# A graph layer kernel on one core: the first tiles reordered, four weight sums moved, two turned tiles moved to SyncE, and two small regroupings

## The chip, the cores and the metric

The kernel runs on one core of a Trainium2 chip. The metric is the device time of one execution in microseconds (us), measured on the slowest core, here the only one. Lower is better.

## What is computed

The layer takes x (1250 nodes of 1024 numbers) and a list of 20,000 edges. Cut to what matters here:

```python
xn = layernorm(x)
h   = relu(xn @ W_self0 + mean_of_neighbours(xn) @ W_neigh0 + b0)
gnn = h @ W_self1 + mean_of_neighbours(h) @ W_neigh1 + b1
q, k, v = relu(xn @ Wq + bq), relu(xn @ Wk + bk), xn @ Wv + bv
mix = (q @ (k.T @ v) / (l * DH), by head) @ Wo + bo       # no softmax: k.T @ v can be summed first
x = x + gnn + mix
x = x + bitlinear(gelu(bitlinear(layernorm(x), w1)), w2)  # weights and activations rounded
```

The mean over neighbours divides by the degree of each node. Weights are scaled by powers of two that come from their norms, so each weight must be read and summed before it is used.

## The kernel before

Nodes are handled in 10 tiles of 128 rows. A float32 product is made from float16 parts: x and each weight are split into a high and a low part (`split`: ScalarE writes the high part, VectorE the low), and a product of one tile with one 1024x1024 weight is 8 steps over k, each of three passes of two 512 wide matmuls, 48 matmuls in all (`product`, line 1683).

The program is written by hand for each engine: the order of the instructions in the source is the order on the engine, and engines wait for each other through named semaphores. SyncE (SP) issues nearly all DMAs, one after the other; a wait on its queue holds all that stands behind it. ScalarE (ACT) issues the DMA transposes.

The head of the program is what the change touches most:

- Tile 0 of x is normalised (`ln_stats`, `ln_xn`), turned by 8 TensorE transposes (`xT_first`, line 1698) into PSUM banks 2 and 3, and copied to `x0T` by ScalarE (line 575, left half) and VectorE (line 964, right half). TensorE multiplies it in float32 with the raw Wk (`k_first`, line 1709), since Wk has no scale yet. The result waits in banks 0 and 1 for `k_t(0)` (VectorE, line 1007).
- Meanwhile ScalarE squares the rows of Wk (line 606), `Wk_total` on TensorE (line 1690) adds them over partitions, `weight_scale` makes the scale, and Wk is split (lines 590 and 971). `k_pe(1)` then follows the splits chunk by chunk, into banks 4 and 5, and `k_pe(2)` goes to banks 0 and 1, so it waits for `k_t(0)`. `k_t` needs the scale of the bias, made by `bias_max` (line 990) and `kv_scale` (lines 995, 922 to 931 and 997).
- Wv goes the same way (`Wv_total`, splits, `v_pe(0)`), then `v_pe(1)` and `kv_sum` (line 1727), which adds k.T @ v over the tiles.
- Tiles 3 and later of x are not turned by TensorE. They are written as `HL` (high part: ScalarE, line 564; low part: VectorE, line 958), and two DMA transposes write them to `XH` (`turn_rows`, line 569). `k_pe(3)` is the first that waits for such a tile.
- Between its other work ScalarE sums all other weights, 8 chunks of 128x1024 for each tile (line 672), which SyncE loads into the four slots of `STREAM` (line 319).

After the k and v products come the q products (line 1803), the count matrix of the edges (line 1868), the neighbour sums (line 1922), the degrees (`deg_pe`, line 1942), and the two bitlinear products (lines 2009 and 2046). The very last product of the program is `f2_product(3, ...)`, 16 matmuls 512 wide, after which VectorE adds them to the output (line 1561, `y_step(p, 8)`) and SyncE writes it out (line 518).

## Time and profile before

| | us |
|---|---|
| median of 3 runs | 1339.29 |
| lowest and highest | 1334.96, 1342.78 |
| the profiled execution, its own time | 1340.48 |
| its span in the profile | 1338.7 |
| TensorE busy in it | 1323.7 (99%) |
| VectorE, ScalarE busy | 855.2 (64%), 463.4 (35%) |

The span runs from the first to the last thing that the profile shows; the profiled execution took 1.8 us more than that. Below, "the chain of waits" is the view that sums who waited for whom, the timeline lists instructions in order of time with the idle time in front of each and what ended it, and the table of windows gives busy times and the granted clock of TensorE in a stretch.

### The profile page before, as it was taken

The page shows a single profiled execution, that of the slowest core. Times are in us where ns is not written, and L with a number is a line of the kernel's source. Part 1 is how long each engine was busy: PE and PEld are TensorE (multiplying, and loading weights), DVE is VectorE, ACT ScalarE, POOL GpSimd, SP SyncE. Part 2 cuts the span into 40 slices and gives each one's busy share as a digit, 9 for nine tenths or more (in the row PEclk, how much of TensorE's full clock was granted, in tenths as well). Part 3 has the DMA queues.
Part 4 walks back from the last instruction along what each step waited for, and adds up shares of the span by engine and source line. Part 5 has one row for each costly group of instructions (what it writes and reads, how often), then busy time and mean ns, then how long its engine had stood idle before and what let it go on. Part 6 is the DMA issues. An engine that isn't in the chain of part 4 may idle for free.

```text
span 1338.7 us, 19417 instructions
## 1 busy us (share of the span) xinstructions
PE 1323.7 (99%) x6642; PEld 630.5 (47%) x6642; DVE 855.2 (64%) x1511; ACT 463.4 (35%) x672; POOL 3.8 (0%) x16
## 2 busy tenths in 40 slices
PE   8989999999999999999999999999999999999999
PEld 4445444555445444444444444444444444444444
DVE  5745452353567754645888966954887658886774
ACT  6665665355411222221112112110100067474460
POOL 0000000000000000000000000000000000000000
PEclk9999999999999999999999999999999999999999
DMA  8298887674235441104776774645555408623523
GB/s 345 64 273 256 292 281 235 243 259 144 103 110 189 145 171 49 33 1 126 205 203 167 204 210 126 220 141 227 182 173 157 141 32 263 160 62 97 126 49 109
DMA packets 173051, 219.94 MB, mean 164 GB/s; under 512 B 93872, under 2 KB 127152, under 8 KB 171696
## 3 DMA queue, kind: packets, MB, share of 16 engines
q1 hardware_dynamic: 128624, 207.95, 47.3%
q10 hardware_dynamic: 44352, 11.02, 5.2%
q8 instruction: 44, 0.72, 0.2%
q14 instruction: 31, 0.25, 0.1%
HBM read 164.41 MB, written 32.51 MB: 147 GB/s over the span
## 4 chain that ended last, share of the span: by engine, by line
PE 94%; DMA 2%; DVE 2%; ACT 1%; issue 0%; SPq 0%; ACTq 0%; DVEq 0%
PE ps L1683 51%; PE ps L1922 13%; PE ps L2009 9%; PE ps L2046 9%; PE ps L1803 8%; PE ps L1868 2%; DMA XH<-HL 1%; DMA S<-in_Wk 1%; PE ps L1727 1%; PE ps L1811 1%; DVE Zb L971 1%; DMA STREAM<-in_w1t 0%; DMA STREAM<-in_w_all 0%; SPq L290 0%; PE ps L1942 0%
## 5 line engine op out<-in xcount | busy, mean ns | idle before, releaser
L1683 PE MATMUL ps<-S,XH 128*128 128x512 f16 x2400 | 526.5, 379 | 0.0
L1683 PEld LDWEIGHTS ps<-S,XH 128*128 128x128 f16 (+1 forms) x2400 | 232.8, 98 | 276.0
L1922 PE MATMUL ps<-Zb,AT 128*128 128x512 f16 x800 | 177.1, 382 | 0.0
L1922 PEld LDWEIGHTS ps<-Zb,AT 128*128 (+1 forms) x800 | 78.6, 98 | 95.4 <-issue 2.3
L1683 PE MATMUL ps<-S,Zb 128*128 128x512 f16 x480 | 106.3, 379 | 0.0
L1683 PE MATMUL ps<-Zb,XH 128*128 128x512 f16 x432 | 97.0, 383 | 7.4 <-DMA XH<-HL 3.4
L1803 PE MATMUL ps<-XH,S 128*128 128x512 f16 (+1 forms) x576 | 102.6, 339 | 0.0
L1229 DVE TENSOR_SCALAR STREAM<-tables,keys 128x320 f16 x240 | 71.5, 298 | 30.1 <-issue 17.7
L1334 DVE SCALAR_TENSOR_TENSOR STREAM<-STREAM,cols 128x1024 fp8e4<-128x1024 f32 x64 | 79.2, 1279 | 0.0
L1803 PEld LDWEIGHTS ps<-XH,S 128*128 128x128 f16 x576 | 56.1, 98 | 47.0 <-issue 2.3
L747 ACT ACTIVATE AT<-ps 128x320 f16<-128x320 f32 x40 | 17.5, 437 | 158.9 <-PE ps L1873 158.9
L672 ACT ACTIVATE STREAM<-STREAM 128x1024 f32<-128x1024 f32 x64 | 66.9, 1046 | 14.2 <-DMA STREAM<-in_w1t 9.2
L1683 PEld LDWEIGHTS ps<-S,Zb 128*128 128x128 f16 x480 | 45.8, 98 | 53.9 <-issue 0.6
L1683 PEld LDWEIGHTS ps<-Zb,XH 128*128 128x128 f16 x432 | 42.3, 99 | 59.9 <-issue 6.3
L1478 DVE TENSOR_TENSOR Zb<-ps,Zb 128x512 f32<-128x512 f32 x60 | 41.3, 689 | 40.0 <-PE ps L2009 27.8
L1231 DVE TENSOR_SCALAR STREAM<-tables,keys 128x128 f16 x240 | 59.7, 249 | 0.3 <-issue 0.3
L852 ACT ACTIVATE Zb<-ps 128x512 f32<-128x512 f32 x60 | 35.1, 594 | 68.0 <-PE ps L2009 41.5
L790 ACT ACTIVATE HL<-TMP 128x1024 f16<-128x1024 f32 x10 | 10.6, 1056 | 137.6 <-DVE TMP L1361 137.6
L590 ACT ACTIVATE S<-SPLIT,cols 128x1024 f16<-128x1024 f32 (+1 forms) x42 | 47.3, 1138 | 29.2 <-issue 20.1
L887 ACT ACTIVATE Zb<-Zb,cols 128x1024 f32<-128x1024 f32 x40 | 46.3, 1230 | 19.7 <-DVE cols L1518 19.7
L977 DVE SCALAR_TENSOR_TENSOR S<-SPLIT,cols,S 128x1024 f16<-128x1024 f32 (+1 forms) x40 | 50.9, 1278 | 0.4 <-ACT S L590 0.2
L1330 DVE TENSOR_SCALAR STREAM<-STREAM,cols 128x1024 fp8e4<-128x1024 f32 x64 | 45.7, 747 | 4.5 <-DMA STREAM<-in_w1t 3.9
(237 smaller groups left out, 1401.2 us busy)
## 6 DMA issues: line engine op xcount, KB each, us to landing
STREAM<-in_w1t SPq DMA_DIRECT2D x64, 512.0 KB, 5.0
STREAM<-in_w2t SPq DMA_DIRECT2D x52, 512.0 KB, 4.4
STREAM<-in_w_all SPq DMA_DIRECT2D x48, 512.0 KB, 6.3
XIN<-in_x SPq DMA_DIRECT2D x20, 512.0 KB, 5.5
SPLIT<-in_Wneigh SPq DMA_DIRECT2D x16, 512.0 KB, 5.9
SPLIT<-in_Wself SPq DMA_DIRECT2D x16, 512.0 KB, 4.4
w1q_scratch<-STREAM SPq DMA_DIRECT2D x16, 512.0 KB, 5.1
w2q_scratch<-STREAM SPq DMA_DIRECT2D x16, 512.0 KB, 3.6
```

What stands on the lines that cost most here:

```text
L590: A(dst, src, ACT.Copy, scale=scale).then_inc(S("split_hi"), 1)
L672: A(STREAM[:, n % 4, :], STREAM[:, n % 4, :], ACT.Square if n < NORMS else ACT.Abs, accum_out=total).then_inc(S("stream_used"), 1)
L887: A(piece, piece, ACT.Identity, bias=col("magic"), scale=at("g_sc", t % 2)).then_inc(S("g_magic"), 1)
L977: V.scalar_tensor_tensor(dst[:, kc, 1, :], SPLIT[:, slot, :], scale, dst[:, kc, 0, :], ALU.mult, ALU.subtract).then_inc(S("split_lo"), 1)
L1229: V.tensor_scalar(hot_m[j][:, bass.ds(r, 1), :], iota_m[:, :], key_m[:, bass.ds(c_ + j, 1)], None, ALU.is_equal)
L1231: one = V.tensor_scalar(hot_s[j][:, bass.ds(r, 1), :], iota_s[:, :], key_s[:, bass.ds(c_ + j, 1)], -float(g * P), ALU.subtract, ALU.is_equal)
L1334: V.scalar_tensor_tensor(made[:, 2 * n:2 * n + 2, :], STREAM[:, n, :].rearrange("p (s n) -> p s n", s=2), col("nthr")[:, w:w + 1], made[:, ...
L1683: last = mm(acc[:, n * BANK:(n + 1) * BANK], left(l, kc), right(kc, r)[:, n * BANK:(n + 1) * BANK], start=(kc == 0 and i == 0), stop=(kc = ...
L1803: last = mm(ps[:, 3 * j * BANK + a:3 * j * BANK + b], Wq_s[:, kc, l, mc], XH[:, r, kc, a:b], start=(kc == 0 and l == 0 and r == 0), stop=( ...
L1922: last = mm(banks(bank + n, 1), AT_tile(t, s), Z[:, r, s, n * BANK:(n + 1) * BANK], start=(s == 0 and r == 0), stop=(s == NT - 1 and r == 1))
L2009: last = mm(banks(F1_BANKS[s][bank], 1), left[:, kc, :], W1[right][:, kc, j * BANK:(j + 1) * BANK], start=(start and kc == 0), stop=(stop ...
L2046: last = mm(banks(bank, 1), left[:, kc, :], W2[right][:, kc, :], start=(start and kc == 0), stop=(stop and kc == HC // 2 - 1), skip_group_ ...
```

## The change

Seven edits in one diff:

1. TensorE's dummy matmuls at the start: 10 rounds of 6 in place of 12. The normalised tile 0 is written in two halves, and each half of the turned tile 0 has a semaphore of its own, so that transposes and the first four steps of `k_first` can start on the left half. The semaphores of the identity matrix are merged.
2. SyncE loads x tile 1 after the fourth chunk of Wk in place of the fifth, and the k bias after x tile 2 in place of between Wk chunks.
3. `xT_first(1)` is before the splits of Wk on ScalarE and VectorE; statistics and normalising of tile 2 move from after splits 3 and 4 to after splits 1 and 2; `xT_first(2)` is directly after the splits on VectorE, before `bias_max(0)` and `kv_scale(0)`; on TensorE the transposes of tile 2 stand before step 3 of `k_pe(1)` in place of step 5.
4. `k_pe(2)` goes to banks 2 and 3 and does not wait for `k_t(0)`; `k_t(1)` is made first and `k_t(0)` second, `v_pe(1)` goes to banks 0 and 1.
5. Tile 3 is normalised on VectorE directly after the splits of Wv, before `v_t(0)`; four of tile 1's weight sums on ScalarE stand before `v_hi(0)`; `v_hi` of tiles 1 and 2 stands before the seventh sum in place of after the eighth. The DMA transposes of tiles 3 and 4 are issued by SyncE, after the load of the next x tile and before the 8 stream loads; those of tile 5 and later stay on ScalarE.
6. The 100 matmuls of `deg_pe` are made in five groups of 20 between steps of `s0_pe(0)` in place of after it.
7. The last product is made as two halves of 256 columns (banks 3 and 4), each added and written out by itself.

```diff
             load_x(0, 0)
             for kc in range(KC):
                 sp.dma_start(raw[:, kc, :], Wk[kc * P:(kc + 1) * P, :]).then_inc(S(f"wk_in{kc}"), 16)
-                if kc == 4:
+                if kc == 3:
                     load_x(1, 1)
-                if kc == 5:
-                    sp.dma_start(b_kv[:, 0, :], bk.partition_broadcast(P)).then_inc(S("bk_in"), 16)
             sp.wait_ge(S("ln_xn"), 1)
             load_x(2, 0)
+            sp.dma_start(b_kv[:, 0, :], bk.partition_broadcast(P)).then_inc(S("bk_in"), 16)
...
+                if turn:
+                    sp.wait_ge(S("ln_hi"), t + 2)
+                    sp.wait_ge(S("ln_lo"), t + 2)
+                    for h in range(2):
+                        sp.dma_start_transpose(XH[:, h, :, tile_of(t + 1)], HL[:, j, h, :])\
+                            .then_inc(S(f"turned{j}"), 16)
...
-            kv_loads(2, 1)
-            kv_loads(3, 0)
+            kv_loads(2, 1, turn=True)
+            kv_loads(3, 0, turn=True)
...
             for kc in range(KC):
                 split(Wv_s[:, kc, 0, :], Wv_raw(kc), at("s", WV))
+            k_hi(0, 0, 1)
+            for n in range(3):
+                weight_sum(1, n)
+            ln_std(3)
+            ln_hi(3, 1)
+            weight_sum(1, 3)
             v_hi(0, 0)
...
+            xT_first(1)
             for kc in range(KC):
                 split(Wk_s[:, kc, :, :], raw[:, kc, :], at("s", WK), kc)
-                if kc == 0:
-                    xT_first(1)
-                if kc == 3:
+                if kc == 1:
                     ln_stats(2, 0)
-                if kc == 4:
+                if kc == 2:
                     ln_xn(2, 0)
+            xT_first(2)
+            bias_max(0)
             kv_scale(0, WK)
-            xT_first(2)
-            k_t(0, "a_kv0", False)
-            k_lo(0, 0)
-            k_t(1, after=False, bank=4)
+            k_t(1, after=False, bank=4, nth=0)
+            square_sum(1, WV)
             bias_max(1)
-            square_sum(1, WV)
+            k_lo(1, 1, 0)
             weight_scale(1, WV)
-            k_lo(1, 1)
+            k_t(0, "a_kv0", False, nth=1)
             for kc in range(KC):
                 split(Wv_s[:, kc, :, :], Wv_raw(kc), at("s", WV), KC + kc)
-                if kc == 1:
-                    kv_scale(1, WV)
+            k_lo(0, 0, 1)
+            ln_stats(3, 1)
+            ln_xn(3, 1)
+            kv_scale(1, WV)
             v_dve(0, 0, early=1)
+            ln_lo(3, 1)
...
-            with pe.Fori(0, 12):
+            with pe.Fori(0, 10):
...
-            k_first({4: lambda: xT_first(1), 5: Wk_total})
-            k_pe(1, 1, ready=0, between={5: lambda: xT_first(2)}, bank=4)
-            k_pe(2, 0, between={4: Wv_total})
+            k_first({(4, 1): lambda: xT_first(1), (5, 1): Wk_total})
+            k_pe(1, 1, ready=0, between={3: lambda: xT_first(2)}, bank=4)
+            k_pe(2, 0, between={5: Wv_total}, bank=2)
+            pe.wait_ge(S("k_t"), 1)
+            v_pe(0, ready=8)
             pe.wait_ge(S("k_t"), 2)
-            v_pe(0, ready=8)
-            v_pe(1, bank=2)
+            v_pe(1, bank=0)
...
-            s0_pe(0)
+            s0_pe(0, {2: lambda: deg_pe(0), 3: lambda: deg_pe(1), 4: lambda: deg_pe(2),
+                      5: lambda: deg_pe(3), 6: lambda: deg_pe(4)})
...
+                    for n in range(2):
+                        part = slice(n * BANK // 2, (n + 1) * BANK // 2)
+                        for kc in range(HC // 2):
+                            last = mm(banks(3 + n, cut=BANK // 2), hid_S4[:, kc, :], W2["B22"][:, kc, part],
+                                      start=(kc == 0), stop=(kc == HC // 2 - 1), skip_group_check=True)
+                        last.then_inc(S("f2_ps"), 1)
```

How the built programs stand, at three places. First VectorE, from its last splits of Wk to the first results of the k products (L971 and L998 are `split`, L966 and L993 the low part of a turned tile, L990 and L1017 `bias_max`, L1007 and L1034 `k_t`, L1012 `k_lo`; the small rows between are `kv_scale`). Before:

```order
L971 SCALAR_TENSOR_TENSOR Zb<-S,cols,Zb 128x1024 x3
L995 SCALAR_TENSOR_TENSOR cols<-cols 128x1
L922 TENSOR_SCALAR cols<-cols 128x1
L923 TENSOR_SCALAR cols<-cols 128x1
L927 RECIPROCAL cols<-cols 128x1
L928 TENSOR_SCALAR cols<-cols 128x1
L997 TENSOR_SCALAR AT<-AT,cols 128x1024
L931 TENSOR_SCALAR cols<-cols 128x1
L966 SCALAR_TENSOR_TENSOR XH<-ps,XH 128x8x128
L1007 SCALAR_TENSOR_TENSOR TMP<-ps,cols,AT 128x1024
L1012 SCALAR_TENSOR_TENSOR AT<-TMP,AT 128x1024
```

The same place in the changed program:

```order
L998 SCALAR_TENSOR_TENSOR Zb<-S,cols,Zb 128x1024 x5
L993 SCALAR_TENSOR_TENSOR XH<-ps,XH 128x8x128
L1017 TENSOR_REDUCE cols<-AT 128x1
L1022 SCALAR_TENSOR_TENSOR cols<-cols 128x1
L945 TENSOR_SCALAR cols<-cols 128x1
L946 TENSOR_SCALAR cols<-cols 128x1
L950 RECIPROCAL cols<-cols 128x1
L951 TENSOR_SCALAR cols<-cols 128x1
L1024 TENSOR_SCALAR AT<-AT,cols 128x1024
L954 TENSOR_SCALAR cols<-cols 128x1
L1034 SCALAR_TENSOR_TENSOR TMP<-ps,cols,AT 128x1024
L1029 TENSOR_REDUCE cols<-NPW 128x1
```

The low part of tile 2 now stands first after the splits; the bias work stands behind it.

Second TensorE, from the end of `k_pe(1)` to the start of `v_pe(0)`, with the semaphores waited for. Before:

```order
L1683 MATMUL ps<-Zb,XH 128x512 [waits split_lo]
L1683 MATMUL ps<-Zb,XH 128x512
L1683 MATMUL ps<-Zb,XH 128x512 [waits ln_lo,ln_hi,k_t]
L1683 MATMUL ps<-Zb,XH 128x512 x23
L1690 MATMUL ps<-cols,squares 128x1 [waits sq]
L1683 MATMUL ps<-Zb,XH 128x512 x24
L1683 MATMUL ps<-S,XH 128x512 [waits split_hi,k_t]
```

The same place in the changed program:

```order
L1719 MATMUL ps<-Zb,XH 128x512 [waits split_lo]
L1719 MATMUL ps<-Zb,XH 128x512
L1719 MATMUL ps<-Zb,XH 128x512 [waits ln_lo,ln_hi]
L1719 MATMUL ps<-Zb,XH 128x512 x29
L1726 MATMUL ps<-cols,squares 128x1 [waits sq]
L1719 MATMUL ps<-Zb,XH 128x512 x18
L1719 MATMUL ps<-S,XH 128x512 [waits split_hi,k_t]
```

The wait for `k_t` in front of `k_pe(2)` is gone, and the sum for Wv stands one step later.

Third SyncE, from the first stream loads on. Before:

```order
L280 DMA XIN<-in_x 128x1024 [waits ln_xn]
L319 DMA STREAM<-in_w_all 128x1024 [waits split_lo] x4
L319 DMA STREAM<-in_w_all 128x1024 [waits stream_used] x2
L319 DMA STREAM<-in_w1t 128x1024 [waits stream_used] x2
L280 DMA XIN<-in_x 128x1024 [waits ln_xn]
L319 DMA STREAM<-in_w_all 128x1024 [waits stream_used] x6
```

The same place in the changed program:

```order
L324 DMA STREAM<-in_w_all 128x1024 [waits split_lo] x4
L324 DMA STREAM<-in_w_all 128x1024 [waits stream_used] x2
L324 DMA STREAM<-in_w1t 128x1024 [waits stream_used] x2
L280 DMA XIN<-in_x 128x1024 [waits ln_xn]
L310 DMA_TRANSPOSE XH<-HL 128x8x128 [waits ln_lo,ln_hi]
L310 DMA_TRANSPOSE XH<-HL 128x8x128
L324 DMA STREAM<-in_w_all 128x1024 [waits stream_used] x6
```

Two transposes, with a wait for both parts of `HL`, stand between the load of x tile 4 and the stream loads of the second tile.

## Rows read from the trace of the kernel before

**Rows 1.** The page: busy us (share of span) of TensorE and VectorE.

```profile
PE 1323.7 (99%) x6642; PEld 630.5 (47%) x6642; DVE 855.2 (64%) x1511; ACT 463.4 (35%) x672; POOL 3.8 (0%) x16
```

**Rows 2.** Chain of waits of TensorE: who was waited for, total us, times, longest.

```profile
PE ps L1683 <- DMA XH<-HL: 3.4, 1, 3.4
PE ps L1683 <- DVE TMP L1007: 2.9, 1, 2.9
PE ps L1709 <- ACT TMP L575: 1.2, 1, 1.2
...
PE ps L1683 <- ACT Zb L590: 0.8, 1, 0.8
```

**Rows 3.** Timeline of TensorE: start us, us, line, operation, count, [idle before <- releaser].

```profile
1.22 5.62 PE L1759 MATMUL ps<-tables 128*128 128x128 f16 x72 [1.22 <-POOL squares L526]
7.47 1.06 PE L1698 MATMUL ps<-squares,TMP 128*128 128x128 f32 x8 [0.64 <-DVE TMP L953]
9.70 7.13 PE L1709 MATMUL ps<-S,TMP 128*128 128x512 f32 x16 [1.16 <-ACT TMP L575]
...
20.14 0.38 PE L1690 MATMUL ps<-cols,squares 128*128 128x1 f32 x2 [0.47 <-DVE cols L1002]
...
25.61 5.34 PE L1683 MATMUL ps<-Zb,XH 128*128 128x512 f16 x24
...
41.92 6.97 PE L1683 MATMUL ps<-Zb,XH 128*128 128x512 f16 x24 [2.87 <-DVE TMP L1007]
...
48.87 5.34 PE L1683 MATMUL ps<-Zb,XH 128*128 128x512 f16 x24
54.05 20.88 PE L1683 MATMUL ps<-S,XH 128*128 128x512 f16 x96
...
91.38 10.52 PE L1683 MATMUL ps<-Zb,XH 128*128 128x512 f16 x48 [3.41 <-DMA XH<-HL]
```

**Rows 4.** Table of windows: us, busy us by engine, granted clock, DMA share, GB/s.

```profile
42.00:45.00 3.00, 3.00 (x8) 1.07 (x9) 1.45 (x2) 3.00 (x6) 0.00 (x0) 0.50 0.01 3
91.40:93.00 1.60, 1.60 (x8) 0.76 (x9) 1.44 (x2) 0.04 (x1) 0.00 (x0) 1.00 1.01 399
```

**Rows 5.** Timeline of VectorE, columns as in rows 3.

```profile
6.51 0.81 DVE L953 TENSOR_SCALAR TMP<-XIN,mv,cols 128x1024 f32<-128x1024 f32 x1
8.57 0.69 DVE L964 COPY TMP<-ps 128x512 f32<-128x512 f32 x1 [1.25 <-PE ps L1698]
...
22.79 1.29 DVE L971 SCALAR_TENSOR_TENSOR Zb<-S,cols,Zb 128x1024 f16<-128x1024 f32 x1 [1.30 <-ACT Zb L590]
...
28.71 1.28 DVE L942 BATCH_NORM_STATS2 st<-XIN 128x6 f32<-128x512 f32 x2
...
33.88 3.67 DVE L971 SCALAR_TENSOR_TENSOR Zb<-S,cols,Zb 128x1024 f16<-128x1024 f32 x3
...
40.59 1.27 DVE L1007 SCALAR_TENSOR_TENSOR TMP<-ps,cols,AT 128x1024 f32<-128x1024 f32 x1
...
72.28 1.23 DVE L958 SCALAR_TENSOR_TENSOR HL<-TMP,HL 128x1024 f16<-128x1024 f32 x1 [1.12 <-ACT HL L564]
```

**Rows 6.** Timeline of ScalarE and, last, the chain that ended last (start, us, what).

```profile
77.40 1.56 ACTq L569 DMA_TRANSPOSE XH<-HL  x1
...
78.98 4.96 ACTq L569 DMA_TRANSPOSE XH<-HL  x1
...
78.98 12.26 DMA XH<-HL
```

**Rows 7.** DMA issues of the whole program: count, median us from issue to landing.

```profile
XH<-HL ACTq DMA_TRANSPOSE x42, 3.6
```

**Rows 8.** Timeline of the program's last us; then landing of the last stores.

```profile
1331.76 3.62 PE L2046 MATMUL ps<-S,XH 128*128 128x512 fp8e4 x16
1335.49 0.75 DVE L1561 SCALAR_TENSOR_TENSOR TMP<-ps,cols,TMP 128x512 f32<-128x512 f32 x1 [2.04 <-PE ps L2046]
out<-TMP SPq DMA_DIRECT2D x2, 256.0 KB, 2.0
```

More of the change, by code:

```diff
@@ L300, in _, with kv_loads @@
             sp.dma_start(col("bq"), bq_cols).then_inc(S("bq_in"), 16)
-            def kv_loads(t, j, first=False, split=False, more=True):
+            def kv_loads(t, j, first=False, split=False, more=True, turn=False):
                 if more:
@@ L659, in kv_act @@
                 if norms:
-                    for n in range(NORMS + KV_MEANS):
+                    for n in range(4 if first else 0, NORMS + KV_MEANS):
+                        if (first or second) and n == 6:
+                            v_hi(t, j)
                         if ln and n == 2:
@@ L664, in kv_act @@
                             ln_hi(t + 2, j)
[L666 to L676 removed]
+                        weight_sum(t, n)
+                if first:
+                    act.wait_ge(S("kv_ps"), 1)
+                    k_hi(2, 0)
+                if not first and not second:
+                    v_hi(t, j)
+            kv_act(1, 1, ln=False, first=True)
             kv_act(2, 0)
@@ L1079, in kv_dve @@
                     ln_lo(t + 2, j)
-                v_dve(t, j, bank=2 if first else 4)
+                if first:
+                    dve.wait_ge(S("v_lo"), 1)
+                v_dve(t, j, bank=0 if first else 4)
             def other_scales(count, ws, norms):
@@ L1733, in k_pe @@
                 if bank == 0:
-                    wait(pe, "k_t", t - 1 if isinstance(t, int) and t == 2 else t)
+                    wait(pe, "k_t", t)
+                    if isinstance(t, int) and t == 3:
+                        pe.wait_ge(S("v_t"), 2)
                 if isinstance(t, int) and t < 3:
@@ L1935, in h_pe, with deg_pe @@
                 s0_pe(t)
-            def deg_pe():
-                for t in range(NT):
+            def deg_pe(g):
+                for t in range(2 * g, 2 * g + 2):
                     for s in range(NT):
```

123 lines of the change are left out of this document (71 added, 52 removed).

## The prediction

> **What bounds the kernel now.** I read the page first: TensorE is busy 1323.7 of the 1338.7 us span [rows 1], so it is the bound, and a change can give back only the 15.0 us in which it stands idle, what it loses at the lower clock, and what lies behind its last matmul. Next, the chain of waits on TensorE [rows 2] says for whom it stands: 3.4 us for the DMA transposes of x tile 3, 2.9 us for `k_t(0)` on VectorE, 1.2 us for the copy of the turned tile 0, and smaller ones for the splits of Wk. The timeline [rows 3] puts all of these in the first 91.4 us. The reader is to see there that from 91.38 on no wait of size is left until the last matmul: what starts earlier at 91.38 ends earlier by as much, if nothing new goes short. Last, the windows [rows 4] show the clock: after the idle 2.87 us at 39 to 42, which follow smaller gaps, the granted clock is 0.50 (1.2 GHz) for 3 us, and 24 matmuls take 6.97 us where the next 24 take 5.34 [rows 3]: 1.6 us lost. After the idle 3.41 us before 91.38, in front of which TensorE had been fully busy, the clock stays at 1.00 (2.4 GHz).
>
> **The change, part by part.** I walk the changed program along TensorE with the durations of before. One step over k of a float16 product is 6 matmuls, 1.30 us (5.2 us for 24); a whole product is 10.4 us.
>
> *Start, dummy matmuls and halves.* `TMP` is normalised in 0.81 us from 6.51 [rows 5]. Half of it takes between 0.41 (half) and 0.69 (the copy of 512 columns [rows 5]); I take 0.45, nearest to its own row. The first transposes then start at 7.1 in place of 7.47; four of the eight take half of 1.06 us [rows 3], the copy of the left half at most the 0.69 us of its neighbour, and with two hand-overs of 0.1 us `k_first` starts at 8.5 in place of 9.70: **-1.2 us**, bounds -0.4 and -1.5. The 12 matmuls fewer before it save nothing: TensorE waits for VectorE there either way, 0.64 us before and about 1 us after. Their price, if the clock fell for want of them, is at most the 1.6 us above.
>
> *k_first.* 16 float32 matmuls, each two records of the trace, at 0.89 us (7.13 us for 8) and one turned tile. Before, it also stood 0.47 us for the sum over Wk [rows 3]. The k bias moves behind Wk in SyncE's queue and `Wk_total` half a step back, so the wait goes. `k_first` ends at 8.5 + 15.9 - 0.5 = 23.9 in place of 25.61: -1.7 in all, with 0.3 us either way for the last Wk chunks.
>
> *k_pe(1).* `Wk_total` is reached at 8.5 + 11 x 0.89 + 0.9 = 19.2. Before, from there (20.14) to VectorE's first split (22.79) went 2.65 us, in which ScalarE makes its high part; now VectorE writes the low part of tile 1 in that gap, which is free. Splits then run from 21.9: 8 x 1.22 us, plus the statistics (1.28), the normalising (0.81) and their small operations (0.5) [rows 5], plus 0.3 of waiting for ScalarE: the last ends at 34.5, and TensorE's last passes at 35.4. Its own work is 23.9 + 10.4 + 0.9 (transposes of tile 2) = 35.2, so the two fit closely; I take 35.5.
>
> *k_pe(2).* Before it started at 41.92, since between the last split (33.88 + 3.67 = 37.55) and `k_t(0)` (40.59 to 41.86) VectorE had 3.04 us of `kv_scale` and the low part of tile 2, and the bias maximum stood ahead of them all. Now only that low part (1.2 us) is waited for, and TensorE still has 0.9 us of its own: k_pe(2) starts at 35.5, **-6.4 us**, of which 1.7 are from above. The gap of 2.87 shrinks to under 0.4, so the clock should hold at 2.4 GHz: k_pe(2) ends at 35.5 + 10.4 + 0.2 = 46.1 in place of 54.05: **-7.95 us**.
>
> *What is late next: Wv.* VectorE after 34.5: 3.04 us, bias maximum about 1.2, k_t(1) 1.2, second bias maximum 1.2, k_lo 1.2: 42.4. `Wv_total` comes at 35.5 + 5 x 1.30 = 42.0, and 2.65 us later, at 44.9, the first low split starts; k_t(0) fits in between. v_pe(0) at 46.1 needs it by 46.9. So no wait, with 0.8 us to spare; bounds 0 and +2.9, the old wait. From there to k_pe(3) is work alone, 91.38 - 3.41 - 54.05 = 33.9 us [rows 3]: 80.0.
>
> *Turned tiles.* Before, both parts of `HL` for tile 3 were ready at 72.28 + 1.23 = 73.5 [rows 5], yet the first transpose was issued at 77.40, behind ScalarE's sums, and held the queue for 1.56 and 4.96 us; the pair landed at 78.98 + 12.26 = 91.24 [rows 6], 13.8 us after the first issue. Now VectorE ends its Wv splits at 44.9 + 9.8 = 54.7; k_lo, statistics, normalising, `kv_scale`, v_t(0), v_lo(0) and the low part of tile 3 follow, with two waits of 1.1 us for ScalarE as in [rows 5]: 10.8 us, so HL is ready at 65.5. SyncE is free by then (its last stream load of tile 1 waits for the fourth sum, about 61). Landing takes between 3.6 us, the median of such DMAs [rows 7], and 13.8; this is the same traffic by kind, so I reckon with 13.8: 79.3, still before 80.0. The wait of 3.41 goes: **-11.35 us** in all at k_pe(3). Tile 4: the sums of tile 2 start late, since SyncE was held 6.5 us, but its HL is ready at about 82, it lands by 96 at the long price, and k_pe(4) is due at 102.3; 6 us to spare.
>
> *Degrees.* 100 matmuls of 2 columns stand between others in place of after them, the same count. Bounds -0.3 and +0.5 (0.1 for each of five groups): 0.
>
> *Last product.* 32 matmuls of 256 columns in place of 16 of 512 have the same columns. The last addition (0.75 us for 512 columns [rows 8]) becomes about 0.48, by 1.27 for 1024 and 0.75 for 512 [rows 5, 8]: -0.27. The store of 256 KB landed in 2.0 us [rows 8]; for half of it I take 1.9: together **-0.35 us**, bounds 0 and -0.8. The Trainium skill (DMA: Bandwidth & Descriptors, Anatomy of one DMA) gives about 2.0 us and the bytes at 436 GB/s for a DMA of its gpsimd path, which would be 0.3 us less for half the bytes and 11.9 in all in place of 11.7; the row's 2.0 us for 256 KB is below the page's 2.6.
>
> Sum: -11.35 - 0.35 = -11.7. The profiled execution took 1340.5, so 1328.8; it stood 1.2 above the median of the runs shown, 1339.29, from which the sum gives 1327.6. I say **1328.2**.
>
> **The rivals.** *A, the turned tile still comes late.* Moving an issue does not make a transfer quicker, and what SyncE gains ScalarE's order may lose. For it: the margin by the long price is 0.7 us. Against: the median landing is 3.6. If tile 3 lands 4 us later than I reckon, 3.4 us stay: 1328.2 + 3.4 = 1331.6. The Trainium skill (DMA: Bandwidth & Descriptors, Issuing engines are not separate DMA queues) says this: all issuers share the same 16 DMA engines, so another issuer saves only issue time; by it the 13.8 us stay and only the earlier issue counts; no row here shows this pair issued by SyncE.
>
> *B, VectorE becomes the bound of the head.* Its work is packed: splits of Wk end within 0.3 us of TensorE's own, Wv's first with 0.8 us to spare. If `v_pe(0)` waits as `k_pe(2)` did, 2.9 us and the 1.6 of the slow clock come back: 1328.2 + 4.5 = 1332.7.
>
> *C, slower: SyncE's queue as a chain.* With transposes and loads in one queue, loads behind a pair land only after it; the sums of the tile wait for them, `ln_hi` of the next tile stands behind the sums on ScalarE, and the next pair behind that. At 13.8 us a pair, tile 4 has 6 us left and tile 5, once more on ScalarE, about none: its sums start when the loads behind tile 4's pair land, near 96, take 14 us with the rest of ScalarE's work, and 110 + 13.8 is 123.8, where k_pe(5) is due at 102.3 + 22.1 = 124.4. If a pair takes X us more, k_pe(5) starts near 3X later. It decides from 3X = 11.7, a pair of 17.7 us; at X = 6 the time is 1328.2 + 18 = 1346. Against it: no pair took over 13.8 in the busiest stretch.
>
> *D, the gain is given back behind 91 us:* another engine was just hidden. The page shows VectorE at 64% and ScalarE at 35% [rows 1]; I give it little. If half is given back, 1328.2 + 5.9 = 1334.1.
>
> **How the numbers follow.** My forecast 0.60, A 0.15, B 0.14, C 0.06, D 0.05. A measurement of this kernel can tell about 0.5%, 6.7 us, so the bound is 1332.6: forecast nearly all, A half (with smaller misses added), B a quarter are beyond it: faster 0.73. Within it the rest of A and B, and D: 0.20. Slower 0.07, C. The range goes from 1323 (all lower bounds, 2.5 us, and the runs' own spread) to 1336 (A and B together are 1336.1) and leaves C and part of D out.
>
> **What would show it.** Right: TensorE's first 128x512 f32 matmul near 8.5; k_pe(2) at 35 to 36 with under 0.5 us of idle time; no window at 0.50 clock near 42; v_pe(0) at 46; transposes from SyncE issued at 65 to 66; k_pe(3) near 80 without a wait; idle time of TensorE before 100 us near 4 us in place of 11. Wrong: a wait of v_pe(0) for a split (B), of k_pe(3) to k_pe(5) for XH (A, C), a total gain under 6 us though k_pe(3) starts 11 us earlier (D), or a clock of 0.50 in k_first.

## The result, and the profile after

| | before | after |
|---|---|---|
| median | 1334.96 | 1326.32 |
| lowest, highest of 5 runs each | 1334.46, 1342.78 | 1326.17, 1326.50 |
| the profiled execution, its own time | 1340.48 | 1326.50 |
| its span | 1338.7 | 1324.7 |

The change makes the kernel faster: 0.9914 of the time before, 95% interval 0.9896 to 0.9932. The 1328.2 forecast stood 1.9 us above what came, and the range held it. The table shows a second thing: the five runs before lie over 8.3 us, the five after over 0.33. So how much is gained depends on which run of before one holds against it. In all comparisons of this study the kernel before ran 64 times: 1334.22 to 1342.78, median 1337.57. Against that median the gain is 11.3 us, against the fastest run 7.9, and between the two profiled executions 14.0. All three are explained below.

The page after, busy time by engine:

```profile
PE 1320.0 (100%) x6646; PEld 632.2 (48%) x6646; DVE 855.0 (65%) x1513; ACT 463.0 (35%) x672; POOL 3.8 (0%) x16
```

TensorE's mean granted clock over the execution is 1.000, where it was 0.997. Against [rows 1] TensorE is busy 3.7 us less with four matmul records more: 16 more in the last product, now cut into 32, and 12 dummy matmuls fewer. The products are the same, and the 60 dummies take more time than the 72 did (6.31 and 5.62 us), so the rest of the work takes 4.4 us less. 3.3 of these are clock, lost before in two stretches at 1.2 GHz (1.6 near 42 us in [rows 3], and 1.7 near 618 us, shown below); the other 1.1 I can't put down to one place. The rest of the 14.0 us is idle time, in front of `k_pe(3)` and in the tail. The chain of waits of TensorE (columns as in [rows 2]; left out is one of 0.4 us that stood there before as well):

```profile
PE ps L1802 <- POOL squares L536: 1.2, 1, 1.2
...
PE ps L1750 <- ACT TMP L642: 0.3, 1, 0.3
PE ps L1737 <- DVE TMP L980: 0.2, 1, 0.2
```

The first is the fill of the table for the dummy matmuls, which stood there before too. The waits for `XH` and for `k_t(0)` of [rows 2] are gone. The timeline of TensorE, beside [rows 3]:

```profile
1.22 6.31 PE L1802 MATMUL ps<-tables 128*128 128x128 f16 x60 [1.22 <-POOL squares L536]
7.36 1.04 PE L1737 MATMUL ps<-squares,TMP 128*128 128x128 f32 x8
8.66 7.99 PE L1750 MATMUL ps<-S,TMP 128*128 128x512 f32 x18 [0.25 <-ACT TMP L642]
...
23.59 4.05 PE L1719 MATMUL ps<-Zb,XH 128*128 128x512 f16 x18
...
28.70 13.11 PE L1719 MATMUL ps<-Zb,XH 128*128 128x512 f16 x60
...
45.67 20.88 PE L1719 MATMUL ps<-S,XH 128*128 128x512 f16 x96
...
79.43 10.52 PE L1719 MATMUL ps<-Zb,XH 128*128 128x512 f16 x48
```

The row at 28.70 is the one to stop at: the last 30 matmuls of `k_pe(1)` and the first 30 of `k_pe(2)` are one group without a gap, so `k_pe(2)` starts near 28.70 + 30 x 0.217 = 35.2, where it started at 41.92. `v_pe(0)` is at 45.67 (was 54.05) and `k_pe(3)` at 79.43 (was 91.38), with no wait. The window where the clock had been 0.50 [rows 4]:

```profile
42.00:45.00 3.00, 3.00 (x15) 1.37 (x14) 2.69 (x6) 2.21 (x3) 0.00 (x0) 1.00 0.00 0
```

VectorE in the head, beside [rows 5]: the two halves of the normalising, the last five splits of Wk with the low part of tile 2 behind them, the first splits of Wv, and the low part of tile 3:

```profile
6.50 0.55 DVE L978 TENSOR_SCALAR TMP<-XIN,mv,cols 128x512 f32<-128x512 f32 x1
6.96 0.54 DVE L980 TENSOR_SCALAR TMP<-XIN,mv,cols 128x512 f32<-128x512 f32 x1
...
27.57 6.06 DVE L998 SCALAR_TENSOR_TENSOR Zb<-S,cols,Zb 128x1024 f16<-128x1024 f32 x5
33.55 1.21 DVE L993 SCALAR_TENSOR_TENSOR XH<-ps,XH 128x1024 f16<-128x1024 f32 x1
...
44.13 4.87 DVE L998 SCALAR_TENSOR_TENSOR S<-STREAM,cols,S 128x1024 f16<-128x1024 f32 x4
...
63.29 1.22 DVE L985 SCALAR_TENSOR_TENSOR HL<-TMP,HL 128x1024 f16<-128x1024 f32 x1
```

The queue of SyncE, beside the ScalarE queue of [rows 6]; the last line is the landing of its four transposes from issue, shortest, median and longest:

```profile
64.59 2.71 SPq L310 DMA_TRANSPOSE XH<-HL  x2
67.35 7.93 SPq L324 DMA_DIRECT2D STREAM<-in_w_all  x6
...
80.10 4.62 SPq L310 DMA_TRANSPOSE XH<-HL  x2
DMA to landing us min/median/max: 3.2/4.3/5.8
```

The pair for tile 3 is issued 0.1 us after its data are ready (63.29 + 1.22). Its two transposes land 3.2 and 3.3 us after their issues (the longer times are tile 4's, 5.4 and 5.8), so it has landed by 69.3, 10 us before `k_pe(3)`.

**Where the other clock loss was.** [rows 4] show one slow stretch. The trace of before has a second, behind the 100 matmuls of the degrees, at 616 us. Timeline of TensorE, then the table of windows there:

```profile
616.01 2.64 PE L1942 MATMUL ps<-one,AT 128*128 128x2 f16 x100
618.51 19.11 PE L1922 MATMUL ps<-Zb,AT 128*128 128x512 f16 x80
```

```profile
618.00:620.00 2.00, 2.00 (x30) 1.06 (x28) 1.17 (x3) 0.00 (x0) 0.00 (x0) 0.67 0.03 8
620.00:622.00 2.00, 2.00 (x6) 0.76 (x5) 1.76 (x8) 0.00 (x0) 0.00 (x0) 0.50 0.01 4
```

TensorE stands idle nowhere here, yet its clock falls to 1.2 GHz. The 80 matmuls take 19.11 us; with the clock at 1.00 the same 80 take 17.43, 1.7 us less. After the change the degrees stand in groups of 20 (timeline of TensorE, the last of the five groups and the same 80 matmuls, then the window behind the groups):

```profile
603.33 0.64 PE L1986 MATMUL ps<-one,AT 128*128 128x2 f16 x20
...
606.56 17.43 PE L1966 MATMUL ps<-Zb,AT 128*128 128x512 f16 x80
```

```profile
606.00:610.00 4.00, 4.00 (x21) 1.98 (x20) 2.90 (x11) 0.00 (x0) 0.00 (x0) 1.00 0.00 0
```

**The tail**, beside [rows 8], the timeline from the last product on:

```profile
1318.39 3.66 PE L2136 MATMUL ps<-S,XH 128*128 128x256 fp8e4 x32
...
1320.41 0.48 DVE L1699 SCALAR_TENSOR_TENSOR TMP<-ps,cols,TMP 128x256 f32<-128x256 f32 x1 [0.34 <-PE ps L2136]
1320.92 2.01 SPq L528 DMA_DIRECT2D out<-TMP  x2
1322.09 0.48 DVE L1699 SCALAR_TENSOR_TENSOR TMP<-ps,cols,TMP 128x256 f32<-128x256 f32 x1 [1.20 <-PE ps L2136]
```

The last matmul ends at 1322.05 and the span at 1324.7: 2.65 us, where before 1338.7 - 1335.38 = 3.32 stood. So the 14.0 us between the two profiles are 11.95 up to `k_pe(3)`, 0.67 in the tail, and 1.4 between them: 1.7 gained by the clock behind the degrees, less 0.3 over the rest of the program.

### The profile page after: what moved, and what is told of

Its sections match the earlier page's. It is cut to its first block, busy times and chain, and to the rows that moved or that the text cites. A ratio compares the mean times of both kernels' runs of the same rounds, so it can differ in the third digit from the quotient of the medians.

```text
span 1324.7 us, 19430 instructions
## 1 busy us (share of the span) xinstructions
PE 1320.0 (100%) x6646; PEld 632.2 (48%) x6646; DVE 855.0 (65%) x1513; ACT 463.0 (35%) x672; POOL 3.8 (0%) x16
## 4 chain that ended last, share of the span: by engine, by line
PE 96%; DVE 2%; DMA 1%; issue 1%; ACT 0%; POOL 0%; DVEq 0%; ACTq 0%; POOLq 0%
PE ps L1719 54%; PE ps L1966 13%; PE ps L2054 8%; PE ps L1847 8%; PE ps L2091 7%; PE ps L1912 3%; PE ps L1768 1%; DMA AT<-Zb 1%; PE ps L1750 1%; PE ps L1855 1%; DVE AM L1531 1%; PE ps L1802 0%; DVE Zb L998 0%; PE ps L2136 0%; DVE Zb L1555 0%
## 5 line engine op out<-in xcount | busy, mean ns | idle before, releaser
L813 ACT ACTIVATE HL<-TMP 128x1024 f16<-128x1024 f32 x10 | 10.6, 1057 | 137.1 <-DVE TMP L1391 137.1
```

## The experiments

My theory: three things that are separate in the text of the change hold each other up in time. The wait for `k_t(0)`, the late sum of Wv and the late turned tile lie one behind the other, so taking one away alone only moves the wait to the next. On top of this sits a random part: after each gap the clock may or may not fall. The rivals: one single edit (the banks, or the SyncE transposes) carries the gain by itself; or it is all clock. Three sets were run, each beside the kernel before on the same chip, the last three runs below on another chip than the first eight. The changed kernel itself ran only in the five runs of the result, so a few tenths of a us between it and a variant may come from the occasion: the median of before was 1334.96 in the result and 1337.61, 1339.11 and 1336.34 in the sets. What no run tries is the new order of banks taken out of the changed kernel, tile 3's early normalising or the new places of tiles 1 and 2 between the splits by themselves, and banks and SyncE's transposes together without the other reorderings.

**The kernel before, once more.** No edit.

> The kernel before, once more, to see a second trace of it. Theory 1 (the time lost in the degrees is the granted clock at 0.50 from about 618.7 to 622, after the 100 matmuls of 2 columns, and it depends on where these fall): 80 matmuls of the first neighbour sum take 18.9 us in a run that has the slow stretch and 17.3 in one that has not, and the fastest runs of before (1334.5) are those that lack one or both slow stretches. Theory 2 (the trace shown was typical): both slow stretches, the wait of 2.9 us and the wait of 3.4 us are there again and the time is 1339 to 1341. A span near 1333 with both slow stretches gone would speak for theory 1.

10 runs from 1335.61 to 1340.38, 1.0001 (0.9985 to 1.0018). Its profile (own time 1337.75) is what matters. Timeline and chain of waits of TensorE:

```profile
41.08 5.35 PE L1683 MATMUL ps<-Zb,XH 128*128 128x512 f16 x24 [2.87 <-DVE TMP L1007]
...
87.06 10.52 PE L1683 MATMUL ps<-Zb,XH 128*128 128x512 f16 x48 [1.12 <-DMA XH<-HL]
```

```profile
PE ps L1727 <- DVE AT L1021: 1.2, 1, 1.2
```

The same gap of 2.87 us as in [rows 3], but here 24 matmuls behind it take 5.35 us and not 6.97: the clock did not fall this time. It did fall behind the degrees again (0.62 from 616 to 620 us, 19.11 us for the 80 matmuls). The wait for the turned tile is 1.1 in place of 3.4, and in its place `kv_sum` waits 1.2 us for VectorE. So the wait and the clock both vary from one execution to the next, with the same program.

59 of the 64 runs of before have their mean granted clock on record. The 13 at 1.000 took 1334.22 to 1336.1 us, the 18 at 0.999 took 1335.19 to 1339.39, and the 28 at 0.997 or less took 1336.55 to 1342.02. So much of the scatter goes with the clock. But it is not all clock: the 13 that lost none of it stand at least 7.9 us above the median of the change.

**The degrees in groups, on the kernel before.**

```diff
-            s0_pe(0)
+            s0_pe(0, {2: lambda: deg_pe(0), 3: lambda: deg_pe(1), 4: lambda: deg_pe(2),
+                      5: lambda: deg_pe(3), 6: lambda: deg_pe(4)})
...
-            deg_pe()
```

> The kernel before with only the degrees in five groups. Theory 1 (grouping avoids a fall of the clock): the window 618 to 622 is at clock 1.00, the 80 matmuls behind take 17.3 us, and the time is 1.5 to 1.8 us under that of before in a run with the slow stretch. Theory 2 (the same work, no gain): within 0.3 us of before.

1337.66 (1333.19 to 1340.00), 0.9997 (0.9981 to 1.0014): nothing that can be told, beneath a spread of 7 us. The clock and the 80 matmuls (17.43 us) came as theory 1 has it. The windows of its profile show the clock at 0.68 behind the `k_t(0)` gap, at 0.66 behind a wait of 2.17 us for `XH`, and at 1.00 from 600 to 620:

```profile
88.00:92.00 4.00, 2.92 (x8) 1.15 (x9) 2.88 (x3) 3.10 (x6) 0.00 (x0) 0.66 1.07 402
...
616.00:620.00 4.00, 4.00 (x21) 1.98 (x20) 1.72 (x7) 0.00 (x0) 0.00 (x0) 1.00 0.00 0
```

The wait for `XH` is news too: behind the transposes' wait the clock can fall as well, and did not in [rows 4] at 91.4.

**The degrees back in one piece, in the changed kernel.** The edit is the reverse of the last one.

> The changed kernel with the degrees after the product again. Theory 1: the clock falls to 0.50 behind the 100 matmuls and the time is 1327.8 to 1328.1, 1.5 to 1.8 above the changed kernel's 1326.3. Theory 2: 1326.3, nothing.

This is the clean test, since the rest of the changed kernel hardly varies: 1326.21, 1327.72, 1327.89, 1328.08. Three of four runs stand 1.4 to 1.8 us above the 1326.3 of the change, and one stands on it. The windows of a run with 1327.89:

```profile
604.00:608.00 4.00, 4.00 (x110) 3.25 (x109) 1.82 (x7) 0.00 (x0) 0.00 (x0) 0.97 0.02 4
608.00:612.00 4.00, 4.00 (x13) 1.42 (x11) 3.62 (x13) 0.00 (x0) 0.00 (x0) 0.60 0.00 0
```

So 100 matmuls of 2 columns in a row cost up to 1.8 us of clock in most executions, and 20 at a time cost none in the profiles at hand.

**The last product whole again, in the changed kernel.**

```diff
-                for n in range(2):
-                    part = slice(n * BANK // 2, (n + 1) * BANK // 2)
-                    for kc in range(HC // 2):
-                        last = mm(banks(3 + n, cut=BANK // 2), hid_S4[:, kc, :], W2["B22"][:, kc, part],
-                                  start=(kc == 0), stop=(kc == HC // 2 - 1), skip_group_check=True)
-                    last.then_inc(S("f2_ps"), 1)
+                f2_product(3, hid_S4, "B22")
```

> The changed kernel with the last product in one piece. Theory 1 (the end is one addition half as wide and one store half as large): 0.6 to 0.8 us above the changed kernel, 1326.9 to 1327.1, the part behind the last matmul 3.3 us in place of 2.65. Theory 2 (the prediction's term): 0.35 above. Theory 3 (the second product's extra weight loads cost as much): no difference.

1326.80 to 1327.11, median 1326.86; 0.9921 (0.9896 to 0.9947) of before. That is 0.54 above the change, a little less than the 0.6 to 0.8 of theory 1. In the timeline the addition takes 0.75 us again where the second half took 0.48:

```profile
1321.97 0.75 DVE L1586 SCALAR_TENSOR_TENSOR TMP<-ps,cols,TMP 128x512 f32<-128x512 f32 x1 [2.04 <-PE ps L2080]
```

0.27 us are the addition; the other 0.3 come from the store of half the bytes: from the end of the last addition to the end of the span it is 2.13 us in the change and 2.46 in the profile of before. The Trainium skill (DMA: Bandwidth & Descriptors, Anatomy of one DMA) would give 0.3 us for the bytes saved, by its fit for the gpsimd path, and this store, issued by SyncE, agrees with it.

**Tiles 3 and 4 turned from ScalarE again, in the changed kernel.**

```diff
-            kv_loads(2, 1, turn=True)
-            kv_loads(3, 0, turn=True)
+            kv_loads(2, 1)
+            kv_loads(3, 0)
...
-                if norms and not first and not second and not third:
+                if norms and not first:
                     xT_act(t + 1, 1 - j)
```

> The changed kernel with the transposes of tiles 3 and 4 on ScalarE again. Theory 1 (place in the order decides: on ScalarE they stand behind tile 1's sums and k_hi(2), so near 73 in place of 64.6, and beside stream loads that are no longer held back): k_pe(3), due at 79.4, waits 3 to 7 us, time 1329.5 to 1334, with a spread of steps of 1.6 us since the wait can let the clock fall. Theory 2 (the gain came from making HL earlier, the issuer does not matter): no wait over 0.5 us, 1326.3 to 1326.8.

1326.91, 1330.85, 1331.41, 1337.50; 0.9930 (0.9903 to 0.9957). The profiled execution is the longest. Its timeline, TensorE first and then ScalarE with its queue:

```profile
110.13 13.26 PE L1719 MATMUL ps<-Zb,XH 128*128 128x512 f16 x48 [7.24 <-DMA XH<-HL]
```

```profile
71.75 5.13 ACTq L589 DMA_TRANSPOSE XH<-HL  x2
77.01 1.06 ACT L573 ACTIVATE STREAM<-STREAM 128x1024 f32<-128x1024 f32 x1 [4.29 <-issue]
```

`HL` is ready at 64.5, but ScalarE gets to the transposes only at 71.75, and stands 4.3 us while they are issued. They land in 6.3 and 7.3 us, and `k_pe(3)` waits 1.1 us for them, not the 3 to 7 expected; the large wait is one tile later. The transpose of tile 4 issued at 88.30 takes 21.7 us to land, and `k_pe(4)` waits 7.2 us and then takes 13.3 us for its 48 matmuls in place of 10.5: a granted clock of 0.50. The run of 1326.91 shows that the price is not paid each time: it is 0.6 to 11.2 us, 4.8 at the median. With SyncE's issue all five runs are free of it. How much of it is the later issue (7.2 us for tile 3) and how much the longer landing, the four runs don't separate.

**The four weight sums back behind `v_hi(0)`, in the changed kernel.**

```diff
             k_hi(0, 0, 1)
-            for n in range(3):
-                weight_sum(1, n)
             ln_std(3)
             ln_hi(3, 1)
-            weight_sum(1, 3)
             v_hi(0, 0)
...
-                    for n in range(4 if first else 0, NORMS + KV_MEANS):
+                    for n in range(0, NORMS + KV_MEANS):
```

> The changed kernel with the four weight sums of tile 1 behind v_hi(0) again; the high part of tile 3 stays in front. Theory 1 (the sums only fill idle time of ScalarE, but SyncE's last load of tile 1 waits for the fourth sum, so the transposes are issued near 66.5 in place of 64.6, and land by 72): no wait at k_pe(3), 1326.3 within 0.2. Theory 2 (they carry part of the gain): k_pe(3) or k_pe(4) waits over 1 us, 1327.5 or more.

1326.48, 1327.52, 1328.21, 1328.79; 0.9913 (0.9890 to 0.9935), 0.2 to 2.5 us above the change. `k_pe(3)` starts at 79.32 as in the change and waits for nothing. But `kv_sum` does, as in the second run of the kernel before. Chain of waits of TensorE:

```profile
PE ps L1765 <- DVE AT L1045: 2.0, 3, 1.0
```

ScalarE's timeline leads further back:

```profile
77.88 1.06 ACT L573 ACTIVATE STREAM<-STREAM 128x1024 f32<-128x1024 f32 x1 [2.79 <-DMA STREAM<-in_w_all]
```

ScalarE stands 2.8 us for a stream load that SyncE could issue only at 73.48, behind the pair for tile 3 (issued at 67.11, and holding the queue for 6.33 us), and that pair itself comes 2.5 us later than in the change, since SyncE's loads ahead of it wait for the sums. I read it as a ring: late sums, late loads, late transposes, again late sums; `v_hi` stands behind the sums, VectorE behind `v_hi`, `kv_sum` behind VectorE. It is rival C's chain, at a small size. So neither theory came as written: no wait at `k_pe(3)` or `k_pe(4)`, and yet a longer time. The edit that I had not priced at all is worth about 1.5 us at the median.

**The start as before, in the changed kernel**: whole normalising, no start on the left half alone, 12 rounds of dummy matmuls, loads in the old order. `Wk_total` stays half a step later, as in the change.

```diff
-                if kc == 3:
+                if kc == 4:
                     load_x(1, 1)
+                if kc == 5:
+                    sp.dma_start(b_kv[:, 0, :], bk.partition_broadcast(P)).then_inc(S("bk_in"), 16)
...
-                first_half = BANK if isinstance(t, int) and t == 0 else 0
+                first_half = 0
...
-                    pe.wait_ge(*((S("x0_left"), 3) if kc < KC // 2 else (S("x0T_right"), 1)))
+                    pe.wait_ge(S("x0_left"), 1)
+                    pe.wait_ge(S("x0T_right"), 1)
```

> The changed kernel with the start as before: 12 rounds of dummy matmuls, tile 0 in one piece, x tile 1 and the k bias loaded where they were. Theory 1 (the start is worth the 1.0 us by which k_first began earlier, 9.70 against 8.66, plus the wait for the sum over Wk): k_pe(1) starts at 24.5 to 25.0 in place of 23.6 and the time is 0.9 to 1.5 us above, 1327.2 to 1327.8. Theory 2 (VectorE's splits bound what follows, so the start is covered): under 0.3 us, 1326.3 to 1326.6.

1327.14 to 1327.49, median 1327.23; 0.9912 (0.9891 to 0.9934). 0.9 us above the change, in every run:

```profile
9.33 3.24 PE L1747 MATMUL ps<-S,TMP 128*128 128x512 f32 x7 [0.83 <-ACT TMP L644]
```

`k_first` starts 0.67 us later than the 8.66 of the change, and `k_pe(3)` 0.64 later (80.07). `k_pe(1)` starts at 24.24, before the 24.5 of theory 1. So the start is worth 0.6 us by the profiles and 0.9 by the medians.

**8 rounds of dummy matmuls in place of 10, in the changed kernel.**

> The changed kernel with 8 rounds of dummy matmuls in place of 10. In the changed kernel's trace these took 105 ns each and ended at 7.53, behind the left half of tile 0 (7.05). Theory 1 (TensorE was held by its own dummy matmuls): they end near 6.3, the transposes start at 7.1, k_first at 8.2 to 8.4, 0.2 to 0.4 us less: 1325.9 to 1326.1. Theory 2 (fewer of them leave the clock at 0.50 into k_first): 1 to 2 us more, 1327.3 to 1328.3.

1326.10 to 1326.72, median 1326.20; 0.9905 (0.9883 to 0.9927): 0.1 us at most. The timeline has an idle stretch in front of the first transposes, and `k_first` starts at 8.53 in place of 8.66:

```profile
1.22 4.35 PE L1802 MATMUL ps<-tables 128*128 128x128 f16 x48 [1.22 <-POOL squares L536]
7.21 1.06 PE L1737 MATMUL ps<-squares,TMP 128*128 128x128 f32 x8 [1.64 <-DVE TMP L978]
```

In the change the dummies last until the transposes begin at 7.36, though the left half is ready at 6.50 + 0.55 = 7.05; here they begin at 7.21. But this is no effect of the 8 rounds that the runs can show: with 10 rounds and the same start, three other variants (the last product whole, the transposes back on ScalarE, the sums back) have `k_first` at 8.53 to 8.56, and with 8 rounds in the last variant of this study it is at 8.72. What is shown is that 8 rounds lose no clock; whether they gain anything is open.

**The order of banks alone, on the kernel before.** The low part of tile 2 first after the splits, `k_pe(2)` to banks 2 and 3 without the wait for `k_t(0)`, `v_pe(1)` to banks 0 and 1.

```diff
-            kv_scale(0, WK)
             xT_first(2)
+            kv_scale(0, WK)
...
-            k_pe(2, 0, between={4: Wv_total})
+            k_pe(2, 0, between={4: Wv_total}, bank=2)
...
-            v_pe(1, bank=2)
+            v_pe(1, bank=0)
```

> The kernel before with one part of the head alone: the low part of tile 2 ahead of kv_scale, k_pe(2) in banks 2 and 3 and without the wait for k_t(0), v_pe(1) in banks 0 and 1. Theory 1 (that wait, and the fall of the clock that it sometimes brings, are what the head gave back): the wait of 2.87 us goes to under 0.3, the clock stays at 1.00 near 42, and the median is 2.5 to 4 us under that of before, if the new lead is not lost at the transposes of tile 3. Theory 2 (it moves on): v_pe(0) or k_pe(3) wait longer by as much and the time is that of before within 1 us.

1338.81 (1335.28 to 1341.91, 12 runs), 1.0009 (0.9995 to 1.0022), beside a median of 1336.34 for before. The largest wait by the old profile but one is taken away, and no gain comes of it. The timeline of TensorE says why:

```profile
33.87 9.23 PE L1683 MATMUL ps<-Zb,XH 128*128 128x512 f16 x42
46.31 0.59 PE L1690 MATMUL ps<-cols,squares 128*128 128x1 f32 x2 [3.21 <-DVE cols L1002]
46.76 6.73 PE L1683 MATMUL ps<-Zb,XH 128*128 128x512 f16 x24
...
90.10 12.21 PE L1683 MATMUL ps<-Zb,XH 128*128 128x512 f16 x48 [2.85 <-DMA XH<-HL]
```

`k_pe(2)` starts without a gap in the row at 33.87. After its first 24 matmuls stands `Wv_total`, and there TensorE waits 3.21 us for `square_sum(1)` (line 1002), which VectorE reaches only behind both `k_t` and `bias_max(1)`: the row of VectorE stands at 46.09. The clock falls at this new gap as at the old one, then once more behind the wait for `XH`. In the change `square_sum(1)` stands in front of `bias_max(1)` and `k_t(0)`, at 39.12, and `Wv_total` one step later.

**SyncE's transposes alone, on the kernel before.** `kv_loads(2, 1, turn=True)` and `kv_loads(3, 0, turn=True)`, with the same new lines as in the change, and no `xT_act` for these two tiles on ScalarE.

> The kernel before with only the transposes of tiles 3 and 4 issued by SyncE. Theory 1 (behind their own queue's loads they land in 4 to 6 us, where ScalarE's landed in 12): issued near 73.7, landed by 80, k_pe(3) does not wait, 1.1 to 5 us under before, the size by what before waits in that run and whether its clock falls. Theory 2 (SyncE's queue is held and the stream loads of tile 2 come late): the sums of tile 2 start 3 us later and k_pe(4) or kv_sum wait over 1 us.

1335.45 (1333.87 to 1339.93, 12 runs), 0.9996 (0.9985 to 1.0007); the medians differ by 0.9 us, which these runs can't tell from nothing. Its profile (own time 1334.51, mean clock 1.000) shows a program that differs from before only in these transposes, and no stretch at a lower clock, so I use it for an account without the clock. TensorE's timeline, and its chain of waits:

```profile
85.46 10.52 PE L1690 MATMUL ps<-Zb,XH 128*128 128x512 f16 x48
```

```profile
PE ps L1690 <- DVE TMP L1014: 2.9, 1, 2.9
PE ps L1734 <- DVE AT L1028: 1.3, 2, 0.8
```

And the landing of the four transposes:

```profile
DMA to landing us min/median/max: 5.3/5.9/6.9
```

The pair for tile 3 is issued at 71.88. The wait for `XH` is gone, in exchange for 1.3 us at `kv_sum`. The pairs land in 5.3 to 6.9 us where those before 100 us took 8.4 to 13.0 in the first profile of before and 9.7 to 10.6 in the second. Against this profile the 8.0 us of the change (1332.7 to 1324.7) are 85.46 - 79.43 = 6.0 up to `k_pe(3)`, 1.3 at `kv_sum` (both waits are behind it) and 0.7 in the tail. The 6.0 are all there at `v_pe(0)` already (51.70 against 45.67); 2.9 of them are the wait for `k_t(0)`, and 1.5 are three waits within `k_pe(1)` (0.81, 0.28 and 0.41), of which the change keeps 0.15. So where banks and order gave nothing by themselves, in the changed kernel the starts show that they give the larger part; no run takes them out of it.

**8 rounds, and the last product cut 384 and 128 columns wide.** The changed kernel, with the second part shorter than the first, so that the addition and store behind the last matmul are smaller.

```diff
-                        part = slice(n * BANK // 2, (n + 1) * BANK // 2)
+                        part = slice(n * 3 * P, 3 * P + n * P)
                         for kc in range(HC // 2):
-                            last = mm(banks(3 + n, cut=BANK // 2), hid_S4[:, kc, :], W2["B22"][:, kc, part],
+                            last = mm(banks(3 + n, cut=(3 - 2 * n) * P), hid_S4[:, kc, :], W2["B22"][:, kc, part],
```

> The changed kernel with 8 rounds of dummy matmuls and the last product as 384 and 128 columns in place of 256 and 256. Theory 1 (the end is the last addition and its store): the last addition takes 0.34 us in place of 0.48 and the store a little less, so 0.15 to 0.3 us under the changed kernel, 1326.0 to 1326.2. Theory 2 (the first part's store now is the one that ends last, or the narrow matmuls cost more): 1326.3 or above.

1325.94 to 1326.37, median 1326.05; 0.9921 (0.9908 to 0.9935). It is 0.15 under 8 rounds alone and 0.27 under the change, but on another chip, so the times alone don't rank the three. The profile does for the end: 2.44 us from the last matmul (1321.86) to the end of the span, where the change has 2.65:

```profile
1321.07 0.62 DVE L1699 SCALAR_TENSOR_TENSOR TMP<-ps,cols,TMP 128x384 f32<-128x384 f32 x1 [1.19 <-PE ps L2136]
...
1321.90 0.35 DVE L1699 SCALAR_TENSOR_TENSOR TMP<-ps,cols,TMP 128x128 f32<-128x128 f32 x1 [0.21 <-PE ps L2136]
```

The last addition is 0.13 us shorter than with equal halves. Smaller cuts gain little: 512, 384, 256 and 128 columns take 0.75, 0.62, 0.48 and 0.35 us, so about 0.2 us of each is fixed.

## Why the prediction came out

*Start: right, less than said.* `k_first` at 8.66 where I had 8.5; 1.04 us in place of 1.2 between the profiles, 0.6 to 0.9 in the experiment. Part of the difference is the profile of before: its `k_first` at 9.70 is the latest of the five profiles with the old start, the others have 9.31 to 9.50. The step that was off is "half of it ... I take 0.45": a half of the normalising takes 0.55. Besides, I expected 1 us of waiting behind the dummies. In the profile after they ran slower than before and filled it, and cost up to 0.15 us; with the last product whole the same 60 took 5.21 us and TensorE waited 0.81, as I had said.

*k_first, k_pe(1), k_pe(2): right.* End of `k_first` 23.6 (said 23.9), last split 33.6 (34.5), `k_pe(2)` 35.2 (35.5), `v_pe(0)` 45.67 (46.1). I had VectorE's and TensorE's ends within 0.3 us of each other. VectorE had about 1.1 us to spare for its last split (33.6, where the last two matmuls of `k_pe(1)`, which read it, start near 34.8), and 0.5 for the low part of tile 2 (33.55 + 1.21 = 34.76 against 35.2). Rival B, the wait for VectorE, did not come: the first low split of Wv is at 44.13, said 44.9 (where 42.0 + 2.65 gives 44.65). But the change does hang on the order of VectorE's small operations, which the banks-alone run shows: with `square_sum(1)` left where it was, the whole gain of the new banks is paid back as a wait of 3.2 us at `Wv_total`. I had walked past this step as "so no wait", rightly, without saying what it rests on.

*The 1.6 us of clock at 42: right for the profile that I read, and not for the median.* In two of the four profiles of a program with this gap (the first of before and the degrees-alone run) the clock fell, in two (the second of before and the SyncE run) it did not. The term belongs to some executions. So does the wait of 3.41, which was 1.1 and 2.2 in others.

*Turned tiles: the wait goes, as said, but the landing was reckoned far too long.* I took 13.8 us for a pair, from [rows 6]. From SyncE the pair of tile 3 took 4.7 us from its first issue, that of tile 4 at most 7.1. So rival A was not near, and rival C, which decides from 17.7 us a pair, had no ground with the sums where the change puts them. The long price belongs to the moment and the queue: the same transposes issued by ScalarE in the changed kernel took 6.3 to 7.3 us for tile 3 and up to 21.7 for tile 4, while over the whole program of before ScalarE's 34 transposes of `HL` land in 3.9 us at the median. My reading is that from SyncE they stand in one queue with the stream loads and are served before these, while from ScalarE they go beside loads that are in flight; the longest landing fell where loads were queued, but no run varied the loads alone, so this is left as argued. The Trainium skill (DMA: Bandwidth & Descriptors, Issuing engines are not separate DMA queues) says that another issuer saves only the issue time; here the landing became shorter too (5.3 to 6.9 against 8.4 to 13.0), so as a forecast for this kernel the rule gave too long a time. But with the issuer the moment of the issue (71.88 against 77.40) and the loads in flight changed as well, so the run does not show that the issuer itself shortens a landing.

*The moved weight sums: a part that I left out of the sum.* I costed ScalarE's new order at nothing. It is worth 0.2 to 2.5 us by the four runs without it. Without it `kv_sum` waits three times for VectorE. That is rival C's chain and rival D's "another engine was just hidden" in one, at a small size, and the edit keeps it away.

*Degrees: the mis-sized term.* "100 matmuls of 2 columns stand between others in place of after them, the same count. Bounds -0.3 and +0.5: 0." It is up to 1.8 us gained, outside the bounds. I had read the windows around the gaps of TensorE and taken for granted that an engine that is never idle keeps its clock. The trace of before had two signs that I passed over: a granted clock of 0.99 in the window from 600 to 800 us, where TensorE is busy throughout, and 19.11 us for the 80 matmuls behind the degrees. Windows of 2 us there show 0.67 and 0.50 at 618 to 622.

*Last product: right sign, -0.54 by the runs and -0.67 between the profiles, where I said -0.35.* The addition was right to the digit (0.48). The store of half the bytes gives 0.3 and not 0.1.

*The sum.* 11.7 was forecast against the profiled 1340.48. Between the profiles it was 14.0: +0.6 up to `k_pe(3)`, +1.4 between there and the tail (1.7 for the degrees' clock, less 0.3 elsewhere), +0.3 in the tail. Against the median of the 64 runs of before it was 11.3, next to the 11.7 forecast. That closeness is in part luck: the terms that I sized too small add 2.3 us, and the profiled execution of before stood 2.9 us above that median, since what I read from it (the clock at 42, the length of the wait for `XH`) exists only in some executions. Against the 1334.96 of the result the gain is 8.6 us, 3.1 less than the 11.7. The time itself missed by 1.9 us, and no luck is in that: from the profiled 1340.48 the sum gives 1328.8, which is 2.3 above the profiled 1326.50 by just the terms sized too small, and I had gone 0.6 down towards the median.

*Small slips in the working.* The lower bounds of the terms add up to 1.35 us (0.3 each at the start, in `k_first` and at the degrees, 0.45 in the last product), not the 2.5 that the lower end of the range is built on. The parts counted as a clear gain add up to at most 0.71, not 0.73. And "idle time of TensorE before 100 us near 4 us" does not fit the sum: before 100 us it was 11.3, and 11.35 us less of time with some 1.6 of clock and 0.9 of dummies in it leaves 2.5. It came out at 1.6.

## What to carry to other kernels

Where waits lie in a row on an engine that is busy 99% of its time, read for each wait what the engine would reach next, and when that will be ready: the new banks by themselves, and SyncE's transposes by themselves, were worth nothing that could be measured, and the whole change, with its small reorderings, the degrees and the tail, was worth 8 to 11 us. Look at the granted clock over the whole span, above all behind long runs of tiny matmuls, and spread those among full ones. Here runs that scattered over 8 us were a sign of gaps behind which the clock may fall, and of waits for transfers; with the gaps gone the time was steady (0.33 us over five runs) as well as short.

Transposes that change their queue on the way, as here from SyncE (tile 4) to ScalarE (tile 5), want care: the Trainium skill (DMA: Bandwidth & Descriptors, Silent corruption: two transposing streams in flight at once) warns of two streams that transpose at the same time. In the profile after they don't meet: SyncE's last pair is issued from 80.10 to 84.72 and lands within 5.8 us, and ScalarE's first is issued at 106.82.
